# Local attention: the additive mask of the even heads is written by TensorE's products, not by a ScalarE copy

## The reference

```python
def local_attention(q, k, v):              # 8 heads of 64, window 64
    bq = q.reshape(b, h, w, WINDOW, d) * QK_SCALE
    bk = k.reshape(b, h, w, WINDOW, d)
    ...
    bk, bv = (look_around(bk), look_around(bv))   # own window and the one before
    sim = jnp.einsum('bhwid,bhwjd->bhwij', bq, bk)
    mask = (i < j) | (i > j + WINDOW) | (j == -1)
    sim = jnp.where(mask, -jnp.finfo(sim.dtype).max, sim)
    attn = jax.nn.softmax(sim, axis=-1)
    out = jnp.einsum('bhwij,bhwjd->bhwid', attn, bv)
```

## Time and profile before

| | before |
|---|---|
| median of 3 runs | 2184.9 us (2182.38 to 2188.41) |
| profiled execution | 2187.15 us, span 2185.4 us |
| PE / DVE / ACT / POOL busy | 2060.7 / 1711.3 / 1570.3 / 1512.8 us |
| ACT's band copies (L869) | 124, 79.2 us, mean 639 ns |
| DVE's band copies (L1032) | 124, 83.8 us, mean 676 ns |
| PE's band products (L644) | 16 |

### The profile page before, as it was taken

The page is one execution under the profiler, slowest core; times in us unless marked ns, Lnnn a source line. Parts: engine busy times, 40 slices in busy tenths (PEclk is TensorE's granted clock), DMA queues, the critical chain, the costliest instruction groups (busy, mean ns, idle before and its releaser), DMA issues.

```text
span 2185.4 us, 53148 instructions
## 1 busy us (share of the span) xinstructions
PE 2060.7 (94%) x18736; PEld 1413.5 (65%) x18752; DVE 1711.3 (78%) x4035; ACT 1570.3 (72%) x4511; POOL 1512.8 (69%) x1837
## 2 busy tenths in 40 slices
PE   6999779999899999899999999999999989999988
PEld 4777547776567777556666656665777756677755
DVE  6787659999568999667777777777999966999965
ACT  3665449999559999536656655666999964999962
POOL 6788758887247777358877777776888733777742
PEclk9999989999999999999999999999999999999999
DMA  4000011122111122121111121210121211111211
GB/s 121 1 1 1 7 21 37 33 45 48 50 27 39 39 47 49 46 72 48 51 48 39 54 56 41 59 28 20 27 44 43 45 48 29 39 39 40 47 36 51
DMA packets 121367, 88.33 MB, mean 40 GB/s; under 512 B 85560, under 2 KB 102160, under 8 KB 118800
## 3 DMA queue, kind: packets, MB, share of 16 engines
q1 hardware_dynamic: 118544, 82.69, 15.8%
q10 hardware_dynamic: 2560, 2.24, 0.4%
HBM read 30.38 MB, written 8.39 MB: 18 GB/s over the span
## 4 chain that ended last, share of the span: by engine, by line
PE 62%; DVE 11%; POOL 10%; issue 6%; ACT 5%; SPq 4%; DMA 2%; POOLq 0%; ACTq 0%; DVEq 0%
PE bank L1367 11%; PE bank L609 7%; PE bank L1378 5%; PE bank L1358 5%; PE bank L676 5%; PE bank L651 4%; PE bank L622 4%; PE bank L664 4%; PE bank L684 3%; PE bank L739 3%; PE bank L616 3%; SPq L475 3%; POOL store L1167 2%; ACT store L863 2%; PE bank L747 2%
## 5 line engine op out<-in xcount | busy, mean ns | idle before, releaser
L1474 ACT ACTIVATE store<-bank 128x512 f32<-128x512 f32 x512 | 287.4, 602 | 200.5 <-PE bank L1367 197.5
L1521 DVE CUSTOM_DVE_ANT_0 store<-bank,store 128x512 f32<-128x512 f32 x512 | 335.7, 689 | 119.4 <-PE bank L1358 66.7
L1594 POOL TENSOR_SCALAR store<-store 128x512 f32<-128x512 f32 x512 | 348.6, 692 | 108.7 <-DVE store L1521 107.0
L863 ACT ACTIVATE store<-bank,store 128x128 f32<-128x128 f32 x1024 | 367.0, 386 | 16.6 <-DVE store L1019 16.2
L1167 POOL TENSOR_TENSOR store<-store 128x512 f32<-128x512 f32 x256 | 320.5, 1274 | 30.7 <-DVE store L1008 27.4
L1180 POOL TENSOR_TENSOR store<-store 128x512 f32<-128x512 f32 x256 | 261.6, 1042 | 112.2 <-ACT store L513 112.2
L1367 PEld LDWEIGHTS bank<-store 128*128 128x128 f32 x2048 | 239.5, 141 | 133.4 <-ACT store L1474 75.8
L1367 PE MATMUL bank<-store 128*128 128x128 f32 x2048 | 298.2, 277 | 0.0
L609 PE MATMUL bank<-store 128*128 128x512 f32 x496 | 234.8, 594 | 3.3 <-DVE store L1008 3.0
L863 ACT ACTIVATION_READ_ACCUMULATOR store<-bank,store 128x1 f32 x1024 | 230.3, 225 | 0.0
L1171 POOL TENSOR_TENSOR store<-store 128x512 f32<-128x512 f32 x128 | 133.1, 1040 | 127.4 <-DVE store L1024 127.4
(11 more groups left out here) (226 smaller groups left out, 4575.5 us busy)
## 6 DMA issues: line engine op xcount, KB each, us to landing
store<-store SPq DMA_DIRECT2D x256, 128.0 KB, 2.4
store<-parts SPq DMA_DIRECT2D x96, 192.0 KB
parts<-store SPq DMA_DIRECT2D x16, 384.0 KB, 3.6
store<-store SPq DMA_DIRECT2D x128, 32.0 KB
store<-store SPq DMA_DIRECT2D x128, 31.8 KB
store<-store SPq DMA_DIRECT2D x32, 127.0 KB
store<-in_L_ffn_wqkv_dram SPq DMA_DIRECT2D x4, 768.0 KB, 4.3
out_dram<-store SPq DMA_DIRECT2D x8, 256.0 KB, 2.4
```

The costliest lines, as they stand in the source:

```text
L863: last = nc.scalar.activation(prob[:, e, b, :], bank[3 + e][:, b * P:(b + 1) * P], ACT.Exp, bias=nmax[:, e, b:b + 1], accum_out=psums[:, e ...
L1474: nc.scalar.activation(AT[:, h % 4, c, :], bank[SCORE_BANKS + (64 * q + 4 * h + c) % TURN_BANKS][:, :], ACT.Exp, scale=-1.0).then_inc(aexp ...
L1521: nc.vector.tensor_tensor_reduce(out=S[:, h % 4, t, :], in0=bank[(64 * q + 4 * h + t) % SCORE_BANKS][:, :], in1=decay[:, off:off + L], sca ...
L1594: nc.gpsimd.tensor_scalar(s_, s_, -1.0, amax[:, h % 4, t:t + 1], ALU.mult, ALU.add).then_inc(shifted_done, 1)
```

## The change

`BAND_BY_COPY` becomes `(1,)`: in every tile PE writes the band of bank 3 (even heads) with the two products of L644, DVE's copy into bank 4 stays, and ACT's `write_band` is gone, with its calls. PE no longer waits on `band_at[0]`. In the listing below the second hunk lies in `transformer_act` and the third in its `attention_sequence`.

```diff
--- before.py
+++ after.py
@@ -46,7 +46,7 @@
 HID = int(P * 4 * 2 / 3)
 HB = [(0, 128), (128, 128), (256, HID - 256)]
 MASKED = -1e25
-BAND_BY_COPY = (0, 1)
+BAND_BY_COPY = (1,)
 
 
 HA, DA = 16, 8
@@ -864,11 +864,6 @@
                                                 bias=nmax[:, e, b:b + 1], accum_out=psums[:, e, b:b + 1])
                 last.then_inc(exp_done, 1)
 
-            def write_band(q, j):
-                act.wait_ge(exp_done, 8 * q + 2 * j + 1)
-                nc.scalar.activation(bank[3][:, :], band_b[:, 0 if j else 2, :, :].rearrange("p b w -> p (b w)"),
-                                     ACT.Copy).then_inc(band_at[0], 1)
-
             def copy_pT(q, j, e):
                 act.wait_ge(pT_done, 8 * q + 2 * j + e + 3)
                 nc.scalar.activation(probT[:, e, :, :].rearrange("p b t -> p (b t)"), bank[5 + e][:, :],
@@ -894,8 +889,6 @@
                         copy_qkT(*((q, j + 1) if j < 3 else (q + 1, 0)))
                     if more or j < 2:
                         copy_v(*ahead)
-                    if more or j < 3:
-                        write_band(*((q, j + 1) if j < 3 else (q + 1, 0)))
                     copy_pT(q, j, 0)
                     if more or j < 2:
                         inverse_lengths(act, *ahead)
```

## The result

The changed kernel takes 2203.03 us as the median of 6 runs, the kernel before 2185.05 us. The ratio on record is 1.0086, with a 95% interval from 1.0074 to 1.0097 (the quotient of the two medians is 1.0082). The change makes the kernel slower by 0.8 to 0.9%; the forecast was 2202.6 us. The single runs of either kernel lie up to 7.5 us apart.

The account below looks back on a forecast made before the run. PE was taken to bound the tile, alone in its second half and through DVE and ACT in the first. 18.2 - 0.5 = +17.7 us on the 2184.9 us median gave 2202.6 us, range 2193 to 2211.

Parts of the forecast that it names:

- Part 1: ACT's queue: 124 copies of 639 ns removed, 0.48 us of queue each; ACT then waits longer for L664: 0.
- Part 2: PE ahead of the scores: two 64x64 products of 512 columns in 124 tiles, 0.19 us per tile (0.10 to 0.25).
- Part 3: PE's waits for qT, the exponentials and DVE's copy, at the added products: none longer than before, 0.
- Part 4: Tiles 1 to 31 of each stage, where the 0.19 us reaches the end: 18.2 - 0.5 = +17.7 us.
- Tiles 2 to 28: Common loop of the four stages: full price in 108 tiles less 12, 96 x 0.19 = 18.2 us.
- The 12 tiles: Last tile of sequences where DVE also normalizes the next inputs: 0.19 us of slack takes the whole price.
- Tiles 29 and 30: Last sequence of a stage: DVE's feed-forward statistics delay the maxima, 0.29 us of slack, price 0.
- tile 31: Last tile of a stage: PE stood 0.34 us for ACT; scores about 0.12 us sooner, -0.5 us in all.
- Hidden products: Rival: slack in the first half of every tile hides the products, 0 to 0.06 us per tile, 2184 to 2190.5; chance 0.05.
- products one after the other: Rival: products don't overlap or scores' weights come after them, 0.44 us a tile, about +45 us, 2230; chance 0.08.
- ACT's queue as the bound: Rival: ACT's in-order queue closes the loop; removing the copy saves up to 0.29 us a tile, -31 us, 2154; chance 0.05.

Follow-up runs that it names:

- an order where the wait is real: Kernel before, with ACT's probT copy of the previous tile's odd heads ahead of the even heads' exponentials and DVE's add ahead of the rotation: 2176.52 us, ratio 0.9959.

## Why the prediction was right

- **ACT's copy was no real wait in a common tile.** Shown: without copy and products the tile stays at 7.94 us. In an order where the wait is real, the scores come 0.05 us after the copy's end.
- **Part 1, the removal from ACT: 0.** Shown by the copy into unused memory: 2202.50 us against the 2203.03 of the changed kernel.
- **Part 2, 0.19 us a tile.** It measured 0.18 us by the period (8.12 to 8.13 against 7.94 to 7.95). That the price is one product's, with the other quarters at the same time, is shown by two, four and twice two products.
- **Part 3, no new wait.** The source view of the changed kernel has nobody who waits for DVE's copy, and the period has no room for one.
- **Part 4, where it reaches the end.** Tiles 2 to 28: full price. The 12 tiles: 8.12 to 8.13 us against 8.13 to 8.16, as worked out. Tiles 29 and 30: from the maxima of one to those of the other there are 8.08 us, and 8.08 before, so the price there is 0. From tile 30's maxima to tile 31's there are 7.13 us in the second stage, 7.29 before, so tile 31 gained 0.16 us, where I had written 0.12: the real wait of 0.35 less the products' 0.19. My sum of 17.7 us stands against 17.1 in the four stages of the profiled execution, 16.2 without the fall of the clock there, and against 18.0 in the medians. That forecast and median are only 0.4 us apart is partly luck: the 95% interval of the ratio allows 16 to 21 us.
- **Three marks that I had set were wrong.** The scores were to start 0.22 to 0.25 us after the first mask product. They are recorded 0.02 us after it. The price is right all the same, since it can be read from the maxima. ACT was to be idle some 0.8 us ahead of the probT copy; it is 0.68, which is the old 0.18 and the copy's 0.48 us of queue, nearly. And the four stages were to be longer by about 4.5 us each: the second and fourth are (4.6, 4.7), but the first and third, which have the 12 tiles, only by 3.5 (without the clock) and 3.4.
- **The rivals.** Hidden products, and products one after the other: the period decides against both. ACT's queue as the bound (2154 us): wrong for this kernel; the order in which it is near the truth had to be made, and even there the change is no gain.

## What to carry to other kernels

Ask of each engine where in the loop its idle tenths lie before you give it work: the same product cost 0.21 us a tile at one place in TensorE's queue and 0.02 at another. A wait that a trace puts down to an engine is real only if the waiter starts right at that engine's end (0.05 us for the scores here, 0.11 for the values product) and later than its own queue would let it. Moving a copy off an engine that then only waits longer gives nothing; what gave 10.5 us was to move one copy on that same engine ahead of work that it doesn't depend on.

## What I had not expected of the hardware

**The clock of TensorE fell in one attention stage of four, after an idle time that was only a little longer.** In the first stage of the profiled execution of the changed kernel, PE's rows of tiles 30 and 31:

```profile
551.35 1.82 PE L676 MATMUL bank<-store 128*64 128x64 f32 x32 [1.55 <-ACT store L869]
553.10 1.12 PE L622 MATMUL bank<-store 128*128 128x128 f32 x4
...
555.25 0.41 PE L644 MATMUL bank<-store 64*64 64x512 bf16 x2
```

The values product takes 1.82 us where it takes 1.15 in the other stages. The stretches, in the same form:

```profile
550.00:551.00 1.00, 0.00 (x0) 0.00 (x0) 0.18 (x1) 1.00 (x6) 0.02 (x1) 1.00 0.00 0
552.00:553.00 1.00, 1.00 (x22) 0.98 (x19) 0.37 (x2) 0.60 (x4) 0.83 (x3) 0.50 0.00 0
555.00:557.00 2.00, 2.00 (x42) 1.63 (x41) 0.43 (x2) 0.60 (x1) 0.00 (x0) 1.00 0.28 64
```

The granted clock was 0.50 (the level of 1.2 GHz) from some point between 551 and 552 to about 555, and then 1.00 (2.4 GHz) again. Just before, PE had been idle for 1.55 us; in the kernel before it was idle 1.25 us at this place, since its scores start later there, and the clock stayed. From tile 30's mask products to tile 31's are 9.01 us in this stage and 8.08 in the second stage: 0.9 us. The first stage of the kernel without the even mask and of the one with ACT's spare copy show the same (9.02 us), while the other three stages of the changed kernel have 1.55 us of idle time there, too, and no fall, and so has the first stage of the kernel with the pair twice (1.56 us). The two kernels with ACT's copy and another order are no clearer: the first of them fell in its third stage alone, the second in all four. So the idle time alone doesn't decide it, and what does is left open. For a reader of such comparisons it means that a few us of difference can be the clock's.

**Recorded starts of small products don't follow the order of the program.** In the kernel with the pair twice, four score products are recorded at 706.87, ahead of the second pair of mask products (707.09), which stands ahead of all of them in the program. Only the quarters of the odd heads were free then, and where all four quarters hold a mask product, as in the earlier trace rows, the scores start 0.21 to 0.25 us on. I read it as products for free quarters that go ahead of those which wait for theirs; the trace doesn't name the product, so this is argued, not shown. The Trainium skill ("TensorE: Matmul & The Clock Gate", Part 3: Packing small matmuls) says that matmuls both start and end in the order of the program, without any reordering; the row of 706.87 does not agree with it.
